# Two transformer layers on one core: key transfers spread over the cross batches, and the last mixture's rows normalised ahead

## Chip, cores, metric

One core of a Trainium2 chip runs the whole kernel in one launch. The metric is device time in microseconds, the median of several runs. The profile is one execution.

## What is computed

Two layers on a residual stream of 4 batches x 512 tokens x 256 features, all in fp32 (the matmuls that need it are done in three passes over a high and a low part). Each sub-layer adds to x what it computes from the normalised x:

```python
x = x + L0_attention(layernorm(x))            # causal, 16 heads of 16
x = x + L0_geglu(layernorm(x), ctx_1024)
x = x + L0_mixture(layernorm(x))              # 8 experts, top 2, one shared
x = x + L1_attention(layernorm(x))            # full, 16 heads of 16
x = x + L1_cross_attention(layernorm(x), ctx_1024)   # softmax over the QUERIES, for each key
x = x + L1_mixture(layernorm(x))              # 8 experts, top 2, width 1024
```

The change concerns the last two. In the cross attention the softmax runs along the query axis, so the sums belong to keys, and each key's value row is divided by its sum before the product with the probabilities. The mixture first needs logits of all 2048 normalised tokens:

```python
logits = x @ gate_w.T        # 2048 x 8
routing_weights, selected = phi_routing(logits)
```

## The kernel before

Five sub-programs (blocks) follow one another with a barrier between them. Layer 1's full and cross attention are one block, `attention(nc, "l1a", ...)`, with eight batches: b = 0 to 3 full, b = 4 to 7 cross. The mixture is `moe(nc, "l1m", ...)`.

**Attention.** The order of work is a list of steps written out by hand: `attention_schedule` yields (step, b, g, j), and each engine runs through this one list and does what it has for each step, in that order; semaphores do the rest. A step that waits holds back all that its engine has behind it. A batch has four groups g of four heads and 32 score steps "S", at = 8g + j. In a cross batch (`cross_slot`) a score step is:
- TensorE (line 937): scores of a head pair, 128 keys x 512 queries, into one of three score buffers; VectorE (`key_max`, L747): two maxima; ScalarE (L814): two exponentials with their sums.
- Every second step ("W"): VectorE inverts four sums (L756), POOL scales 64 value columns with them (`scale_v`, L612), and some steps later TensorE multiplies probabilities and scaled values ("PV", L962).

Beside these, a slot prepares the next batch: normalisation ("LN1" statistics and, on POOL, the power of the variance; "LN2" normalised rows on VectorE, L653, and on POOL the output bias added to x, `bias`, L575), projections into queries, keys and values ("PREP", "EVAC"), and stacking. Scores are computed with three fp32r operands stacked on the partitions (high, high, low), so each head's 16 rows of queries and keys are copied three times by DMA within on-chip memory: queries by SP's queue ("STACK", L516, 12 DMAs a group), keys by POOL's queue ("KEYS", `stack`, L586, 3 DMAs a head, 12 a group). A group's stack may be overwritten once the scores of the same group of the batch before are done.

In the cross batches the KEYS of the next batch's groups 0, 1 and 2 stand at steps 19 to 30, and group 3's at steps 0 to 3 of the batch itself.

**Mixture.** `moe_schedule` is such a list too. In layer 1 it begins with fillers ("IDLE": `keep_warm`, L98, products of ones that nobody reads), then, batch by batch, "LN1"/"LN2" (DVE L1853, L1859, L1865; POOL L1722, L1725), "TURN" (TensorE transposes the rows, L1959, ScalarE copies them; SP stores them for the later gather) and "LOGITS" (L1969), with fillers in between. Then VectorE routes: L2116 is its first instruction, and all of the rest depends on it. The normalised rows `xn` lie in `raw13`, the buffer that the experts' weights come into later.

## Time and profile before

| | us |
|---|---|
| median of 3 runs | 1621.8 (1618.25 to 1626.14) |
| the profiled execution's own time | 1623.72 |
| its span | 1621.9 |
| busy TensorE / VectorE / ScalarE / POOL | 1440.5 / 1178.2 / 899.5 / 627.7 |
| layer 1's cross batches | 950 to 1173 |
| start of layer 1's mixture | 1185.5 |

The span is from the first to the last instruction of the profiled execution. Shares of the whole say little here, since each block has another limit; what counts is which engine is waited for in the two stretches at the end of the table.

### The profile page before, as it was taken

What the parts mean: (1) busy time and instruction counts of PE and PEld (TensorE: products, weight loads), DVE (VectorE), ACT (ScalarE), POOL (GpSimd) and SP (SyncE); (2) the same over time, 40 slices, a digit from 0 to 9 for tenths busy, and PEclk for the clock granted to TensorE, in tenths of its full rate; (3) what the DMA queues carried; (4) which work ended last, traced back from release to release, by engine and by line L of the source; (5) the groups of instructions that cost most, each with busy time, mean ns of one, the idle gap of its engine ahead of it and who ended that gap; (6) DMA issues with size and microseconds to landing.
All of it is one profiled execution on the core that took longest, in us unless ns stands there. A gap on an engine that the chain in (4) does not pass through costs nothing. (4 is left out here: it accounts for less than half of the span.)

```text
span 1621.9 us, 30209 instructions
## 1 busy us (share of the span) xinstructions
PE 1440.5 (89%) x9918; PEld 995.4 (61%) x9918; DVE 1178.2 (73%) x2499; ACT 899.5 (55%) x1704; POOL 627.7 (39%) x917
## 2 busy tenths in 40 slices
PE   7899998989899999689999988988756899999996
PEld 3455454569899998333434332333244899999996
DVE  4767662554778888478878758888858688888884
ACT  1455553223256666046666687878812576767673
POOL 6445430010235655546445546457113232333221
PEclk8899998998999999779999998999987999999998
DMA  6223320120259886533223323223034677887872
GB/s 167 61 47 58 60 41 27 54 102 21 105 166 254 254 238 172 134 81 60 52 46 68 60 53 80 50 57 76 1 105 131 210 236 238 240 237 234 250 231 43
DMA packets 104553, 194.59 MB, mean 120 GB/s; under 512 B 30448, under 2 KB 55920, under 8 KB 101456
## 3 DMA queue, kind: packets, MB, share of 16 engines
q1 hardware_dynamic: 70864, 153.31, 30.1%
q0 software_dynamic: 33024, 38.97, 13.8%
q8 instruction: 79, 1.29, 0.3%
...
q10 hardware_dynamic: 512, 0.40, 0.1%
...
## 5 line engine op out<-in xcount | busy, mean ns | idle before, releaser
L814 ACT ACTIVATE l1a_sb_probs<-l1a_s_ps,l1a_sb_kmax 128x512 f32<-128x512 f32 x256 | 172.5, 707 | 26.7 <-DVE l1a_sb_kmax L747 25.9
L747 DVE TENSOR_REDUCE l1a_sb_kmax<-l1a_s_ps 128x1 f32<-128x512 f32 x256 | 160.7, 677 | 34.1 <-PE l1a_s_ps L937 33.2
L712 DVE TENSOR_REDUCE l1a_sb_mx<-l1a_s_ps 128x2 f32<-128x1024 f32 x128 | 153.3, 1218 | 38.5 <-PE l1a_s_ps L898 38.4
L820 ACT ACTIVATE l1a_sb_probs<-l1a_s_ps 128x1024 f32<-128x1024 f32 x128 | 130.1, 1024 | 80.0 <-PE l1a_s_ps L937 79.7
L586 POOL DMA_DIRECT2D l1a_sb_kst<-l1a_sb_hi x252 | 124.7, 499 | 101.4 <-PE l1a_s_ps L937 96.3
L937 PEld LDWEIGHTS l1a_s_ps<-l1a_sb_qst,l1a_sb_kst 49*128 49x128 f32 (+1 forms) x512 | 48.7, 189 | 168.6 <-issue 96.7
L707 DVE CUSTOM_DVE_ANT_0 l0a_sb_seen<-l0a_s_ps,l0a_sb_above 128x128 f32<-128x128 f32 (+3 forms) x256 | 113.5, 487 | 52.2 <-PE l0a_s_ps L898 51.8
L2026 PE MATMUL l1m_g_ps<-l1m_sb_rows_hi,l1m_sb_hi 128*128 128x256 f32 x512 | 146.8, 287 | 0.0
L2026 PE MATMUL l1m_g_ps<-l1m_sb_rows_lo,l1m_sb_hi 128*128 128x256 f32 x512 | 145.3, 284 | 0.0
L2026 PE MATMUL l1m_g_ps<-l1m_sb_rows_hi,l1m_sb_lo 128*128 128x256 f32 x512 | 145.3, 284 | 0.0
L937 PE MATMUL l1a_s_ps<-l1a_sb_qst,l1a_sb_kst 49*128 49x512 f32 (+1 forms) x512 | 126.3, 503 | 18.5 <-ACT l1a_sb_probs L814 16.5
L1759 POOL DMA_INDIRECT out_x<-l1m_sb_late,l1m_sb_add_to x39 | 64.5, 1654 | 187.8 <-DVE l1m_sb_late L1946 182.9
L1898 DVE TENSOR_TENSOR l1m_sb_lo<-l1m_sb_raw,l1m_sb_hi 128x512 fp32r<-128x512 f32 x184 | 119.5, 692 | 18.8 <-ACT l1m_sb_hi L1809 17.4
L820 ACT ACTIVATE l0a_sb_probs<-l0a_s_ps 128x1024 f32<-128x1024 f32 (+3 forms) x128 | 88.8, 701 | 63.7 <-PE l0a_s_ps L907 63.4
L2026 PE MATMUL l0m_g_ps<-l0m_sb_rows_hi,l0m_sb_hi 128*128 128x256 f32 x384 | 113.7, 296 | 7.4 <-DVE l0m_sb_rows_lo L1892 6.8
L2026 PE MATMUL l0m_g_ps<-l0m_sb_rows_hi,l0m_sb_lo 128*128 128x256 f32 x384 | 111.7, 291 | 0.0
L2026 PE MATMUL l0m_g_ps<-l0m_sb_rows_lo,l0m_sb_hi 128*128 128x256 f32 x384 | 111.6, 291 | 0.0
L1809 ACT ACTIVATE l1m_sb_hi<-l1m_sb_raw 128x512 fp32r<-128x512 f32 x184 | 104.7, 621 | 0.0
L2026 PE MATMUL l1m_y_ps<-l1m_sb_hi,l1m_sb_h_hi 128*128 128x256 f32 x312 | 91.0, 292 | 11.2 <-DVE l1m_sb_lo L1904 7.2
L2026 PEld LDWEIGHTS l1m_g_ps<-l1m_sb_rows_hi,l1m_sb_hi 128*128 128x128 f32 x512 | 98.8, 193 | 0.8 <-DVE l1m_sb_rows_lo L1892 0.6
L2026 PEld LDWEIGHTS l1m_g_ps<-l1m_sb_rows_hi,l1m_sb_lo 128*128 128x128 f32 x512 | 98.8, 193 | 0.0
L2026 PEld LDWEIGHTS l1m_g_ps<-l1m_sb_rows_lo,l1m_sb_hi 128*128 128x128 f32 x512 | 98.6, 193 | 0.0
...
## 6 DMA issues: line engine op xcount, KB each, us to landing
...
l1a_sb_qst<-l1a_sb_hi SPq DMA_DIRECT2D x256, 32.0 KB, 2.2
...
l0a_sb_qst<-l0a_sb_hi SPq DMA_DIRECT2D x128, 32.0 KB, 2.3
l1a_sb_qst<-l1a_sb_lo SPq DMA_DIRECT2D x128, 32.0 KB, 2.2
...
```

The lines of the kernel that those rows point to most:

```text
L586: pool.dma_start(in_stack(kst, p, e, n), in_part(source, i, p, e)).then_inc(kstacked[p], 16)
L707: ins = dve.tensor_tensor_reduce(seen[:, j % 2, e, 0:last], buffer("A", b, g, j)[:, e, 0:last], above[:, T - last:T], 1.0, -3e38, ALU.add, ...
L712: dve.tensor_reduce(mx[:, g, qt, 2 * p:2 * p + 2], buffer("A", b, g, j)[:, :, :], AX.X, ALU.max).then_inc(a_max.sem, 1)
L747: dve.tensor_reduce(kmax[:, n % 4, e:e + 1], buffer("S", b, g, j)[:, e, :], AX.X, ALU.max, negate=True).then_inc(kmax_done.sem, 1)
L814: ins = act.activation(probs[:, n % 8, e, :], at[:, e, :], ACT.Exp, bias=kmax[:, n % 4, e:e + 1], accum_out=zsum[:, n % 4, e:e + 1])
L820: act.activation(probs[:, n % 8, :, c0:T], at[:, :, c0:T], ACT.Exp, scale=SCALE).then_inc(exp_done.sem, 1)
L937: ins = pe.matmul(at[:, e, c0:T], kst[rows, p, kt * P:(kt + 1) * P], qst[rows, p, c0:T], start=True, stop=not causal)
L1759: pool.indirect_dma_start(total, bass.IndirectOffsetOnAxis(ap=at, axis=0), y[:, e % 2, t, :], None, compute_op=ALU.add).then_inc(stored[e ...
L1809: ins = act.activation(two_chunks(hi, s % 2, f), raw13[:, s % n13, f, n, :, :], ACT.Copy)
L1898: ins = dve.tensor_tensor(two_chunks(lo, s % 2, f), raw13[:, s % n13, f, n, :, :], two_chunks(hi, s % 2, f).bitcast(F32), ALU.subtract)
L2026: ins = pe.matmul(at, s, m, start=n == 0, stop=n == len(passes) - 1)
```

## The change

1. **Keys.** For the cross batches that follow a cross batch (b = 5, 6, 7), group 0's key stack is issued by SP (new `keys_stack`, own semaphores `kfirst_sp`), between its query stacks 0 and 1. Group 1's heads stay on POOL, at steps 19 to 22 of the batch before; groups 2 and 3 go to steps 4, 6, 8, 9 and 10 to 13 of the batch itself.
2. **Rows ahead.** In the last cross batch, at steps 2, 10 and 18, VectorE takes the statistics of batches 0, 1 and 2 of x (which are final there), and POOL computes the power and the normalised rows, written where the mixture expects them (`raw13` is now allocated ahead of the attention).
3. **Mixture.** Its schedule normalises batch 3 alone, starts with 6 fillers in place of 12, and has none of the others (7, 4, 4 and 4); transpositions and logits are ordered 0, 1 | 0 | 2 | 1, 2 | 3 | 3. `Tally` only moves up in the file.

```diff
@@ cross_slot
         if at == 19 and nxt is not None:
             yield "STACK", nxt, 0, 0
+            yield from keys(nxt, 0)
             yield "STACK", nxt, 1, 0
...
-        if at < GH:
-            yield "KEYS", b, NG - 1, at
-        if at >= 19 and nxt is not None and at < 19 + 3 * GH:
-            yield "KEYS", nxt, *divmod(at - 19, GH)
+        if nxt is None and at in (2, 10, 18):
+            yield "AHEAD", at // 8, 0, 0
+        if turned:
+            if at < GH:
+                yield "KEYS", b, NG - 1, at
+        elif b > 0 and kinds[b - 1] == "cross" and at in (4, 6, 8, 9, 10, 11, 12, 13):
+            yield "KEYS", b, *((2, (4, 6, 8, 9).index(at)) if at < 10 else (3, at - 10))
+        if nxt is not None and 19 <= at < 19 + GH:
+            yield "KEYS", nxt, 1, at - 19
@@ attention: SP
+            def keys_stack(b, g, head):
+                if not by_sp(b, g):
+                    return
+                p, e = 2 * g + head // 2, head % 2
+                hi_done.wait(sp, b, 1)
+                lo_done.wait(sp, b, 1)
+                s_ready.wait(sp, b - 1, 8 * g + 7)
+                for n, source in enumerate((hi, hi, lo)):
+                    sp.dma_start(in_stack(kst, p, e, n), in_part(source, 1, p, e)).then_inc(kfirst_sp[p], 16)
@@ attention: POOL
-                if b == 0 and g == 0 and e:
+                if b == 0 and g == 0 and e or by_sp(b, g):
                     return
...
+            def norm_ahead(i, *_):
+                if normed is None:
+                    return
+                stats_ahead.wait(pool, i, 2 * NT - 1)
+                pool.tensor_tensor(rstd_a[:, i, 0, :], mv_a[:, i, :, 1], const["eps"][:, :], ALU.add
+                                   ).then_inc(rstd_ahead.sem, 1)
+                rstd_ahead.wait(pool, i, 0)
+                pool.tensor_tensor(rstd_a[:, i, 1, :], rstd_a[:, i, 0, :], const["minus_half"][:, :], ALU.pow
+                                   ).then_inc(rstd_ahead.sem, 1)
+                rstd_ahead.wait(pool, i, 1)
+                for t in range(NT):
+                    pool.tensor_scalar(normed[:, i, t, :], x[:, i * NT + t, :], mv_a[:, i, t, 0:1],
+                                       rstd_a[:, i, 1, t:t + 1], ALU.subtract, ALU.mult).then_inc(normed_ahead.sem, 1)
@@ attention: VectorE
+            def stats_of(i, *_):
+                if normed is None:
+                    return
+                x_added.wait(dve, B + i, 1)
+                for t in range(NT):
+                    dve.bn_stats(stats_a[:, i, t, :], x[:, i * NT + t, :]).then_inc(stats_ahead.sem, 1)
+                stats_ahead.wait(dve, i, NT - 1)
+                dve.memset(nothing[:, :], 0.0)
+                for t in range(NT):
+                    dve.bn_aggr(mv_a[:, i, t, :], stats_a[:, i, t, :]).then_inc(stats_ahead.sem, 1)
@@ moe_schedule, layer 1 (AHEAD = 3)
-    yield "IDLE", 20 if shared else 12, 0
-    yield "LN1", 0, 0
-    yield "LN1", 1, 0
-    yield "LN2", 0, 0
-    yield "TURN", 0, 0
-    yield "LN1", 2, 0
-    yield "LN2", 1, 0
+    yield "IDLE", 20 if shared else 6, 0
...
-        yield "IDLE", 7, 0
+        for b in range(AHEAD, B):
+            yield "LN1", b, 0
+            yield "LN2", b, 0
+        yield "TURN", 0, 0
         yield "TURN", 1, 0
         yield "LOGITS", 0, 0
-        yield "IDLE", 4, 0
-        yield "LN1", 3, 0
-        yield "LN2", 2, 0
         yield "TURN", 2, 0
         yield "LOGITS", 1, 0
-        yield "IDLE", 4, 0
-        yield "LN2", 3, 0
+        yield "LOGITS", 2, 0
         yield "TURN", 3, 0
-        yield "LOGITS", 2, 0
-        yield "IDLE", 4, 0
         yield "LOGITS", 3, 0
@@ moe
+        def normed(eng, b):
+            if b >= ahead:
+                xn_done.wait(eng, b - ahead, NT - 1)
```

What the lists of instructions say, at three places. First POOL, from the end of b = 4 into b = 5: `vscaled` are the scaled values, `kst` the key stacks, `l1a_sb_v` the values' bias, `x_sb` with `l1a_sb_bo` the output bias on x (sizes are partitions x columns). Before:

```order
L612 TENSOR_TENSOR l1a_sb_vscaled<-l1a_sb_v,l1a_sb_rzsum 128x4x16
L622 TENSOR_TENSOR l1a_sb_v<-l1a_sb_v,l1a_sb_bv 128x512
L586 DMA l1a_sb_kst<-l1a_sb_hi 16x512 x2
L586 DMA l1a_sb_kst<-l1a_sb_lo 16x512
L586 DMA l1a_sb_kst<-l1a_sb_hi 16x512 x2
L586 DMA l1a_sb_kst<-l1a_sb_lo 16x512
L612 TENSOR_TENSOR l1a_sb_vscaled<-l1a_sb_v,l1a_sb_rzsum 128x4x16
L575 TENSOR_TENSOR x_sb<-x_sb,l1a_sb_bo 128x1024
L586 DMA l1a_sb_kst<-l1a_sb_hi 16x512 x2
L586 DMA l1a_sb_kst<-l1a_sb_lo 16x512
L612 TENSOR_TENSOR l1a_sb_vscaled<-l1a_sb_v,l1a_sb_rzsum 128x4x16
L586 DMA l1a_sb_kst<-l1a_sb_hi 16x512 x2
```

and in the change:

```order
L654 TENSOR_TENSOR l1a_sb_vscaled<-l1a_sb_v,l1a_sb_rzsum 128x4x16
L664 TENSOR_TENSOR l1a_sb_v<-l1a_sb_v,l1a_sb_bv 128x512
L654 TENSOR_TENSOR l1a_sb_vscaled<-l1a_sb_v,l1a_sb_rzsum 128x4x16
L617 TENSOR_TENSOR x_sb<-x_sb,l1a_sb_bo 128x1024
L654 TENSOR_TENSOR l1a_sb_vscaled<-l1a_sb_v,l1a_sb_rzsum 128x4x16 x2
L628 DMA l1a_sb_kst<-l1a_sb_hi 16x512 x2
L628 DMA l1a_sb_kst<-l1a_sb_lo 16x512
L654 TENSOR_TENSOR l1a_sb_vscaled<-l1a_sb_v,l1a_sb_rzsum 128x4x16
L628 DMA l1a_sb_kst<-l1a_sb_hi 16x512 x2
L628 DMA l1a_sb_kst<-l1a_sb_lo 16x512
L654 TENSOR_TENSOR l1a_sb_vscaled<-l1a_sb_v,l1a_sb_rzsum 128x4x16
```

The transfers that stood between the scalings are gone from here; the first ones left stand behind the bias on x and two further scalings.

Second POOL, in b = 7 of the change around step 10 (before, only scalings stand here):

```order
L654 TENSOR_TENSOR l1a_sb_vscaled<-l1a_sb_v,l1a_sb_rzsum 128x4x16
L628 DMA l1a_sb_kst<-l1a_sb_hi 16x512 x2
L628 DMA l1a_sb_kst<-l1a_sb_lo 16x512
L672 TENSOR_TENSOR l1a_sb_rstd_a<-l1a_sb_mv_a,const_eps 128x4
L675 TENSOR_TENSOR l1a_sb_rstd_a<-l1a_sb_rstd_a,const_minus_half 128x4
L679 TENSOR_SCALAR l1m_sb_raw<-x_sb,l1a_sb_mv_a,l1a_sb_rstd_a 128x256 x4
L628 DMA l1a_sb_kst<-l1a_sb_hi 16x512 x2
L628 DMA l1a_sb_kst<-l1a_sb_lo 16x512
L654 TENSOR_TENSOR l1a_sb_vscaled<-l1a_sb_v,l1a_sb_rzsum 128x4x16
L628 DMA l1a_sb_kst<-l1a_sb_hi 16x512 x2
L628 DMA l1a_sb_kst<-l1a_sb_lo 16x512
L628 DMA l1a_sb_kst<-l1a_sb_hi 16x512 x2
```

Add, power and four normalisations stand ahead of the transfers of steps 10 to 12 and of the scalings of steps 11 and 13.

Third TensorE, from the first instruction of layer 1's mixture: `const_ones_b` are fillers, `l1m_t_ps` transpositions, `l1m_y_ps` logits (written x8 here, each of 16 passes in the trace). Before:

```order
L98 MATMUL l1m_g_ps<-const_ones_b 128x512 x12
L1959 MATMUL l1m_t_ps<-const_ident,l1m_sb_raw 128x128 x8
L98 MATMUL l1m_g_ps<-const_ones_b 128x512 x7
L1959 MATMUL l1m_t_ps<-const_ident,l1m_sb_raw 128x128 x8
L1969 MATMUL l1m_y_ps<-l1m_sb_router,l1m_sb_late 128x8 x8
L98 MATMUL l1m_g_ps<-const_ones_b 128x512 x4
L1959 MATMUL l1m_t_ps<-const_ident,l1m_sb_raw 128x128 x8
L1969 MATMUL l1m_y_ps<-l1m_sb_router,l1m_sb_late 128x8 x8
L98 MATMUL l1m_g_ps<-const_ones_b 128x512 x4
L1959 MATMUL l1m_t_ps<-const_ident,l1m_sb_raw 128x128 x8
L1969 MATMUL l1m_y_ps<-l1m_sb_router,l1m_sb_late 128x8 x8
L98 MATMUL l1m_g_ps<-const_ones_b 128x512 x4
```

and in the change:

```order
L112 MATMUL l1m_g_ps<-const_ones_b 128x512 x6
L2019 MATMUL l1m_t_ps<-const_ident,l1m_sb_raw 128x128 x16
L2029 MATMUL l1m_y_ps<-l1m_sb_router,l1m_sb_late 128x8 x8
L2019 MATMUL l1m_t_ps<-const_ident,l1m_sb_raw 128x128 x8
L2029 MATMUL l1m_y_ps<-l1m_sb_router,l1m_sb_late 128x8 x16
L2019 MATMUL l1m_t_ps<-const_ident,l1m_sb_raw 128x128 x8
L2029 MATMUL l1m_y_ps<-l1m_sb_router,l1m_sb_late 128x8 x8
```

All fillers but the first six are gone, the first transpositions are 16 in a row, and the second logits 16.

## Rows read from the trace of the kernel before

**Rows 1.** Stretches, cross batches: busy us (instructions) by engine, clock (1.00 is full), DMA.

```profile
core 0: us, PE busy (x) PEld busy (x) DVE busy (x) ACT busy (x) POOL busy (x), PEclk, DMA share, GB/s
...
1006.86:1024.94 18.08, 12.64 (x68) 4.99 (x72) 12.49 (x26) 13.51 (x40) 14.92 (x28) 0.81 0.35 90
1063.40:1082.95 19.55, 12.74 (x68) 5.01 (x72) 13.54 (x26) 13.75 (x40) 16.36 (x30) 0.83 0.35 84
1024.94:1037.65 12.71, 12.34 (x70) 4.49 (x68) 12.54 (x24) 11.63 (x35) 0.89 (x3) 1.00 0.07 15
...
1120.95:1135.90 14.95, 12.16 (x60) 4.14 (x64) 10.21 (x20) 13.38 (x40) 11.64 (x25) 0.77 0.30 67
1135.90:1151.55 15.65, 13.57 (x66) 5.01 (x65) 11.14 (x23) 11.48 (x35) 0.88 (x3) 0.78 0.01 2
1151.55:1161.69 10.14, 7.51 (x46) 2.59 (x50) 9.99 (x21) 9.73 (x30) 1.17 (x4) 1.00 0.00 0
```

**Rows 2.** Waits, 950 to 1175 us: who waited <- for whom: us in total, times, longest.

```profile
PE l1a_o_ps L962 <- POOL l1a_sb_vscaled L612: 13.9, 8, 3.2
```

**Rows 3.** Timeline, POOL: start us, us, line, operation, tiles, count.

```profile
1006.02 1.05 POOL L586 DMA_DIRECT2D l1a_sb_kst<-l1a_sb_hi  x2
...
1007.57 0.30 POOL L612 TENSOR_TENSOR l1a_sb_vscaled<-l1a_sb_v,l1a_sb_rzsum 128x64 f32<-128x64 f32 x1
...
1012.25 0.31 POOL L612 TENSOR_TENSOR l1a_sb_vscaled<-l1a_sb_v,l1a_sb_rzsum 128x64 f32<-128x64 f32 x1
```

**Rows 4.** Timeline, PE; in brackets the idle time before and its releaser.

```profile
1008.02 1.06 PE L962 MATMUL l1a_o_ps<-l1a_sb_probs,l1a_sb_vscaled 128*32 128x512 f32 x8 [1.86 <-POOL l1a_sb_vscaled L612]
...
1012.70 1.93 PE L962 MATMUL l1a_o_ps<-l1a_sb_probs,l1a_sb_vscaled 128*32 128x512 f32 x8 [2.73 <-POOL l1a_sb_vscaled L612]
```

**Rows 5.** Timeline, DVE, the same stretch.

```profile
1015.40 1.29 DVE L747 TENSOR_REDUCE l1a_sb_kmax<-l1a_s_ps 128x1 f32<-128x512 f32 x2 [2.72 <-PE l1a_s_ps L937]
```

**Rows 6.** Timeline, DVE, where the mixture's logits are read.

```profile
1205.60 0.29 DVE L2116 TENSOR_TENSOR l1m_sb_lg<-l1m_y_ps,l1m_sb_rbias 128x128 f32<-128x128 f32 x1 [7.61 <-PE l1m_y_ps L1969]
```

**Rows 7.** Groups, POOL, 950 to 1174 us: count, busy us, mean ns of one, idle before.

```profile
L575 POOL TENSOR_TENSOR x_sb<-x_sb,l1a_sb_bo 128x1024 f32<-128x1024 f32 x2 | 4.7, 2350 | 0.0
L554 POOL TENSOR_TENSOR l1a_sb_rstd<-l1a_sb_rstd,const_minus_half 128x4 f32<-128x4 f32 x2 | 2.1, 1032 | 0.2
```

**Rows 8.** Groups, DVE, 1185 to 1206 us.

```profile
L1853 DVE BATCH_NORM_STATS2 l1m_sb_stats<-x_sb 128x6 f32<-128x256 f32 x16 | 5.6, 408 | 4.3 <-PEq L304 4.3
...
L1859 DVE BATCH_NORM_AGGREGATE l1m_sb_mv<-l1m_sb_stats 128x2 f32<-128x6 f32 x16 | 1.5, 156 | 0.2
```

**Rows 9.** Timeline, PE, two projections of b = 7.

```profile
1133.43 1.99 PE L989 MATMUL l1a_m_ps<-l1a_sb_wout,l1a_sb_ox 128*128 128x256 f32 x8
...
1145.27 3.78 PE L989 MATMUL l1a_m_ps<-l1a_sb_wout,l1a_sb_ox 128*128 128x256 f32 x8
```

**Rows 10.** Timeline, PE, head of layer 1's mixture.

```profile
1185.49 5.09 PE L98 MATMUL l1m_g_ps<-const_ones_b 128*128 128x512 bf16 x12 [4.99 <-PEq L304]
...
1196.83 1.04 PE L1959 MATMUL l1m_t_ps<-const_ident,l1m_sb_raw 128*128 128x128 f32 x8
1197.70 1.85 PE L1969 MATMUL l1m_y_ps<-l1m_sb_router,l1m_sb_late 128*128 128x8 f32 x16
1199.41 1.02 PE L98 MATMUL l1m_g_ps<-const_ones_b 128*128 128x512 bf16 x4
1200.27 1.04 PE L1959 MATMUL l1m_t_ps<-const_ident,l1m_sb_raw 128*128 128x128 f32 x8
```

**Rows 11.** Timeline, PE, logits of three batches in layer 0's mixture.

```profile
371.68 7.69 PE L1969 MATMUL l0m_y_ps<-l0m_sb_router,l0m_sb_xnT 128*128 128x8 f32 x48
```

**Rows 12.** Stretches around those logits; columns as in rows 1.

```profile
371.06:374.47 3.41, 3.41 (x33) 3.41 (x31) 1.26 (x2) 1.23 (x2) 0.00 (x0) 1.00 0.00 0
374.47:377.89 3.42, 3.42 (x18) 3.42 (x18) 0.12 (x1) 0.00 (x0) 0.00 (x0) 0.50 0.00 0
```

**Rows 13.** Stretches, head of layer 1's mixture; columns as in rows 1.

```profile
1190.00:1196.00 6.00, 5.63 (x42) 4.20 (x41) 5.92 (x27) 2.17 (x4) 2.66 (x5) 0.98 1.07 366
```

More of the change, by code:

```diff
@@ L87, in wait, with __init__ @@
             eng.wait_ge(self.sem, value)
+class Tally:
+    def __init__(self, sem, per=1):
+        self.sem, self.per = sem, per
+    def wait(self, eng, n, step=0):
+        value = n * self.per + step + 1
+        if value > 0:
+            eng.wait_ge(self.sem, value)
 CHUNK = (0, 2, 1, 3)
+AHEAD = 3
 def keep_warm(pe, at, const, n):
@@ L288, in attention_schedule, with attention @@
         yield "ADD", b, g, j
-def attention(nc, tag, x, const, stages):
+def attention(nc, tag, x, const, stages, normed=None):
     kinds = [kind for kind, _ in stages for _ in range(B)]
@@ L359, in attention @@
         nothing = sb("nothing", [P, 1])
+        if normed is not None:
+            stats_a, mv_a, rstd_a = sb("stats_a", [P, AHEAD, NT, 6]), sb("mv_a", [P, AHEAD, NT, 2]), sb("rstd_a", [P, AHEAD, 2, NT])
         one_row = sb("one_row", [1, T], F32R)
@@ L408, in attention @@
         x_biased = steps("x_biased", 1)
+        stats_ahead, rstd_ahead, normed_ahead = (Tally(sem(n), per) for n, per in (
+            ("stats_ahead", 2 * NT), ("rstd_ahead", 2), ("normed_ahead", NT)))
         kmax_done = steps("kmax_done", 0, 2 * 8 * NG)
@@ L460, in product, with by_sp @@
             return m_ps[:, :] if b else buffer("PREP", b, use, 0)[:, 0, :]
+        kfirst_sp = [sem(f"kfirst_sp{p}") for p in range(2)] if has_cross else None
         STACKED = 6 * 16
+        def by_sp(b, g):
+            return g == 0 and b > 0 and kinds[b - 1] == "cross"
         def kstack_in(eng, b, p):
+            if by_sp(b, p // 2):
+                eng.wait_ge(kfirst_sp[p], (b - B) * STACKED)
+                return
             eng.wait_ge(kstacked[p], (b + 1) * STACKED - (STACKED // 2 if p < 2 else 0))
@@ L541, in _ @@
                              ).then_inc(ones_in, 16)
-            run({"STACK": stack, "LN1": before_batch, "CTX": context, "M": rows})
+            run({"STACK": stack, "KEYS": keys_stack, "LN1": before_batch, "CTX": context, "M": rows})
         @block.gpsimd
@@ L1254, in halves_to @@
     return sum(halves(n) for n in range(e % 2, e + 1, 2))
-class Tally:
-    def __init__(self, sem, per=1):
-        self.sem, self.per = sem, per
-    def wait(self, eng, n, step=0):
-        value = n * self.per + step + 1
-        if value > 0:
-            eng.wait_ge(self.sem, value)
 ALL, TOKENS, WEIGHTS = slice(0, 5), slice(0, 2), slice(2, 5)
@@ L1496, in sem @@
             return ctx.enter_context(nc.semaphore(f"{tag}_{name}"))
-        raw13, raw2 = sb("raw13", [P, n13, NF, 2, CC, 2 * P]), sb("raw2", [P, n2, FC, D])
+        if shared:
+            raw13 = sb("raw13", [P, n13, NF, 2, CC, 2 * P])
+        raw2 = sb("raw2", [P, n2, FC, D])
+        ahead = 0 if shared else AHEAD
         hi1, lo1, hi3, lo3 = (sb(n, [P, 2, CC, width], F32R) for n in ("hi1", "lo1", "hi3", "lo3"))
@@ L1861, in normal @@
             def normal(b, _):
-                ln_stats.wait(dve, b, 2 * NT - 1)
-                ln_rstd.wait(dve, b, 1)
+                ln_stats.wait(dve, b - ahead, 2 * NT - 1)
+                ln_rstd.wait(dve, b - ahead, 1)
                 for t in range(NT):
@@ L1954, in turn @@
             def turn(b, _):
-                xn_done.wait(pe, b, NT - 1)
+                normed(pe, b)
                 for c in range(CC):
@@ L2273, in build @@
         moe(nc, "l0m", x, const, of("l0m"), 512, phi=False, shared=True)
-        attention(nc, "l1a", x, const, [("full", of("l1a")), ("cross", of("l1x") | context)])
-        moe(nc, "l1m", x, const, of("l1m"), 1024, phi=True, shared=False, out=out)
+        raw13 = ctx.enter_context(nc.sbuf_tensor("l1m_sb_raw13", [P, 1, 4, 2, CC, 2 * P], F32))
+        normed = raw13[:, 0, :, :, :, :].rearrange("p f n c d -> p f (n c) d")
+        attention(nc, "l1a", x, const, [("full", of("l1a")), ("cross", of("l1x") | context)], normed)
+        moe(nc, "l1m", x, const, of("l1m"), 1024, phi=True, shared=False, out=out, raw13=raw13)
 def rope_factor():
```

31 lines of the change are left out of this document (19 added, 12 removed).

## Prediction

> **What bounds the kernel now.** I read the profile in this order: busy time and clock by stretch, the waits, the timelines of single engines, and the groups of instructions for prices.
>
> The change touches two places of layer 1: the four cross batches of attention (b = 4 to 7, from 950 us to 1173 us; each is 32 steps of scores, in four quarters of 8) and the first 20 us of the mixture (from 1185.5 us). In a cross batch VectorE and ScalarE share the bound: a quarter that nothing disturbs (from 1024.94 us) takes 12.71 us, of which DVE is busy 12.54 and ACT 11.63 [rows 1]. The first quarters of b = 5 and b = 6 take 18.08 and 19.55 us with the same DVE and ACT work (12.49 and 13.54 us of DVE), and there POOL is busy 14.92 and 16.36 us against 0.89 us in the quiet quarter [rows 1]. The waits say who is late: TensorE waits 13.9 us for POOL's scaled values [rows 2]. The timeline gives the chain: POOL works without a pause on key transfers, each issue some half a microsecond, so that one scaling of 0.3 us stands at 1007.57 us behind three issues and the next only at 1012.25 us [rows 3]. TensorE, in its own order, stands 1.86 us and then 2.73 us before the product that reads it [rows 4]; the scores queued behind that product are late, and DVE stands 2.72 us [rows 5]. Note that the first wait of 1.86 us starved nobody: some 2 us are hidden by the three score buffers. In these stretches the granted clock is 0.81 and 0.83, where the quiet quarter has 1.00 [rows 1].
>
> At the head of the mixture nothing but TensorE and the normalisation runs: DVE gets the logits at 1205.60 us, 20.1 us after the start, and had stood 7.61 us for them; the whole routing follows from there [rows 6]. So this piece is on the path with its full length.
>
> **Part 1, keys.** For b = 5, 6, 7 group 0's 12 issues go to SP, and groups 2 and 3 (24 issues) go from steps 27 to 3 to steps 4 to 13; group 1 goes four steps earlier. SP then issues 60 stack transfers in a batch where it had 48, behind query stack 0 and ahead of query stacks 1 and 2. At about 0.6 us of issue each (the estimate is from the half microsecond of POOL's [rows 3], taken higher) that is 36 us in a batch of 50 us or more, and group 1's queries are wanted 8 steps into the next batch: I cost SP at nothing; its cover is the 14 us left.
> POOL's queue in the first steps becomes: scaling, the bias on x, two scalings. The bias waits for DVE's normalised rows and takes 2.35 us [rows 7]; the scaling behind it comes about 1 us late, less than what is hidden. So I take both first quarters to the undisturbed length. DVE there: 8 steps of 1.27 us (10.14 us for the 8 steps of the last batch's third quarter, which holds nothing else [rows 1]) and the normalisation of 2.2 us, 12.3; I take 13.0, since the quiet quarters need 12.7.
> - b = 5: 18.08 to 13.0, -5.1 us. b = 6: 19.55 to 13.0, -6.5 us.
> - b = 7, first quarter: 14.95 us now [rows 1]; without the stall 10.1 to 10.7.
> Steps 8 to 13 now hold six heads, 6 x 1.44 us of issue and 3 x 0.3 us of scaling = 9.5 us, beside about 8.5 us of DVE: POOL is 1 us late at most, again hidden.
>
> **Part 2, rows of three batches normalised in b = 7.** DVE gains at steps 2, 10 and 18 four statistics of 0.41 us and four aggregates of 0.16 us (issued closely, together 1.85 us, as at the mixture's head) [rows 8]: 5.6 us on the engine that bounds. POOL gains the add, a power of 1.03 us [rows 7] and four normalisations of 128x256. The trace has none of these on POOL. Below they are bounded by the scaling of 64 elements, 0.3 us [rows 3], above by the bias of 1024 elements, 2.35 us [rows 7]; I take 0.6 us, a quarter of the latter, since 256 elements are a quarter. A block on POOL is then 0.2 + 1.03 + 2.4 = 3.7 us, and the scaling behind it 2.5 us late; at step 10 one head's transfers follow, so there it is about 4 us late. I put 1 us on that.
> - b = 7, first quarter: 10.2 + 1.85 = 12.1, from 14.95: -2.9 us.
> - second: DVE 10.2 + two additions to x of 0.6 + 1.85 = 13.3 us. Now it takes 15.65 us at clock 0.78, since a projection of 1.99 us at full clock took 3.78 us at half [rows 9]. That loss of some 4 us may or may not come again; TensorE will be less busy there than before, so I keep it: 17.5, +1.9 us.
> - third: 10.14 to 12.0, +1.9 us. Fourth: as before.
> Sum of the attention: -5.1 - 6.5 - 2.9 + 1.9 + 1.9 + 1.0 = -9.7 us. Bounds: -15 (no half-clock stretch in b = 7, POOL never late) and -3 (two more such stretches of 3 to 4 us).
>
> **Part 3, head of the mixture.** Now the first transposition waits for DVE and POOL (statistics, power, normalisation), and 12 fillers of together 5.09 us keep TensorE running. The change starts transposing after 6 fillers and has no filler after that. At full clock a batch costs: transpositions 0.87 us, logits 1.71 us, fillers 0.86 us (differences of starts) [rows 10]. The new chain is 6 fillers at half clock (half of 5.09, so 2.5), four times (0.87 + 1.71) = 10.3, and one wait for ScalarE's copy before the last logits, 0.85 (its place was under a filler): 13.7 us at full clock, against 20.1. But the clock starts at half, and the logits do not hold it: in layer 0 the same logits, three batches in a row, ran from 371.68 us at full clock up to 374.47 and at half clock from there though TensorE was 100% busy, and took 7.69 us; 2.8 us of it at full clock are 1.6 batches, so the other 1.4 took 4.9 us, 3.5 us a batch [rows 11, 12]. All at half: 2.5 + 4 x 1.74 + 4 x 3.5 + 0.85 = 24.3 us, +4.2. Every microsecond at full clock takes one off. The clock rose some 4.9 us after the start before (0.98 from 1190.00 us on [rows 13]); I let it do the same, and fall some 3 us after logits begin to dominate (at 6.0 us), so 4 us at full: 20.3 us, and call the piece +0.2. The normalisation of the fourth batch (done 5 us after the start) and the stores of rows lie beside this.
> Here a rule speaks against the change. The Trainium skill, page "TensorE: Matmul & The Clock Gate", part 4 on the transposition, says that transpositions don't count as TensorE activity in the way matmuls do, so that the full clock doesn't engage on them. By that, the head would be all at half clock, the first rival below. The trace neither proves nor refutes it: in the mixture's head transpositions always stand next to fillers.
>
> **Sum.** -9.7 + 0.2 = -9.5 us. The profiled execution took 1623.7 us (span 1621.9), so it would take 1614.2. The median of the three runs is 1621.8, 1.9 below it: 1612.3, say 1612. A measurement of this kernel tells about 0.5%, 8 us, from no change, so this stands close to that bound.
>
> **The rivals.**
> - *The head stays at half clock throughout* (+4.2 instead of +0.2): for it, the logits' fall and the absence of fillers; against it, that TensorE has no pause in the first 6 us of the new chain, 6 fillers and two batches' transpositions. Time 1616. Chance 0.17.
> - *The head holds the full clock from 4.9 us on*: 4.9 us at half do 4.9 us of cold work, the rest is halved: 24.3 - 0.85 - 4.9 = 18.5, halved 9.3; 15.1 us, -5.0. For it, that each batch's transpositions interrupt the logits. With it -14.5 us, 1607; if b = 7 escapes its half-clock stretch, 1603. Chance 0.15.
> - *The stall stays* (the change doesn't do what it says): the late scaling is then due to the bias on x, which waits for DVE's rows in the same place, and not to the transfers. Against it: the scaling at 1007.57 stood ahead of that bias and was late already [rows 3]. Then only part 2's additions, +3 to +5, against some relief at b = 7: 1621. Chance 0.08.
> - *Slower: POOL's normalisations block the scalings of b = 7.* If one takes not 0.6 but up to the 2.35 us of the upper bound, a block is 0.2 + 1.03 + 9.4 = 10.6 us; less the 3 us hidden, TensorE and then DVE stand 7.6 us, three times: +23 us in place of the +1.0, sum +12.5, 1634. It turns the forecast into no gain from about 1.5 us a normalisation. For it, a power over 4 elements takes 1.03 us, so POOL's prices aren't by elements alone; against it, both tensor operations shown scale with elements. Chance 0.08.
> - The forecast itself has 0.52.
>
> **Numbers.** The forecast's own range is 1605 to 1619 (bounds of part 2 and the half-clock stretches). With the rivals up to a fifth left out: 1603 to 1621. Faster by over 0.5% (below 1613.7): six tenths of the forecast, all of the second rival, a fifth of the first and a little for a lucky b = 7: 0.55. Slower: the POOL rival and a little of the others, 0.09. The rest, 0.36.
>
> **What would show it.** In the profile after: POOL's share in the first quarters of b = 5 and 6 falls from 15 us to about 5, TensorE's wait for the scaled values from 13.9 us to 3 or less, and those quarters take 13 us. In b = 7 three statistics blocks of 1.85 us on DVE, POOL's normalisations at 0.6 us each. From the mixture's start to DVE's reading of the logits some 20 us, with the clock's share telling which of the three cases of the head it was. It is wrong if TensorE still waits over 5 us for the scaled values, if DVE stands more than 3 us behind any of the three blocks, or if the head is under 17 us.

## The result, and the profile after

The changed kernel takes 1628.99 us (median of 20 runs, 1620.96 to 1635.57) against 1620.78 us for the kernel before (20 runs, 1614.35 to 1630.9). The ratio is 1.0046 with a 95% interval of 1.0032 to 1.0059: about 7.5 us slower. Forecast were 1612 us, 9.5 us faster. The profiled execution took 1631.8 us (span 1630.0, mean clock 0.93).

The table splits the two profiled spans at the same places (the start of each cross batch on VectorE, its last maximum, TensorE's first instruction in the mixture, the reading of the logits), in us:

| piece | before | after | difference | forecast |
|---|---|---|---|---|
| up to b = 4 | 949.93 | 948.82 | -1.1 | 0 |
| b = 4 | 56.93 | 56.90 | 0 | 0 |
| b = 5 | 56.54 | 53.32 | -3.2 | -5.1 |
| b = 6 | 57.55 | 54.09 | -3.5 | -6.5 |
| b = 7 | 52.56 | 71.58 | **+19.0** | +1.9 |
| end of attention to mixture | 11.98 | 8.92 | -3.1 | 0 |
| head of the mixture | 20.10 | 20.86 | +0.8 | +0.2 |
| the rest | 416.32 | 415.54 | -0.8 | 0 |
| span | 1621.9 | 1630.0 | +8.1 | -9.5 |

So the keys' part brought less than forecast, and b = 7 took back more than all other pieces gained together. The stretches of the changed kernel, with the columns of [rows 1]; the first two are the first quarters of b = 5 and 6, the other four are all of b = 7:

```profile
1005.72:1020.57 14.85, 11.82 (x64) 4.84 (x64) 11.67 (x26) 13.39 (x40) 7.96 (x14) 0.89 0.34 80
1059.05:1075.17 16.12, 14.69 (x68) 5.83 (x64) 11.61 (x25) 14.73 (x43) 8.61 (x15) 0.68 0.34 82
1113.13:1132.52 19.39, 13.66 (x60) 4.93 (x63) 11.87 (x29) 14.26 (x42) 12.76 (x20) 0.65 0.22 46
1132.54:1154.59 22.05, 12.81 (x66) 4.71 (x61) 12.78 (x32) 10.78 (x31) 14.82 (x25) 0.77 0.13 26
1154.59:1172.17 17.58, 10.17 (x46) 3.45 (x50) 11.66 (x31) 11.90 (x35) 7.47 (x11) 0.71 0.00 1
1172.17:1184.71 12.54, 10.43 (x58) 2.81 (x58) 11.23 (x22) 9.82 (x29) 0.88 (x3) 0.86 0.00 0
```

POOL's 14.92 and 16.36 us in the first two have become 7.96 and 8.61, and the wait of [rows 2] is gone there: that part of the chain was read rightly. In b = 7 POOL's time stands in its place, and all four quarters show a clock below full. What the profile puts down as TensorE's waits for scaled values lies in b = 7 alone (5.66 us at its step 10, the rest at its end):

```profile
PE l1a_o_ps L1031 <- POOL l1a_sb_vscaled L654: 7.8, 4, 5.7
```

POOL's groups over the cross batches (columns of [rows 7]):

```profile
L679 POOL TENSOR_SCALAR l1m_sb_raw<-x_sb,l1a_sb_mv_a,l1a_sb_rstd_a 128x256 f32<-128x256 f32 x12 | 14.6, 1226 | 0.3
...
L675 POOL TENSOR_TENSOR l1a_sb_rstd_a<-l1a_sb_rstd_a,const_minus_half 128x4 f32<-128x4 f32 x3 | 3.1, 1034 | 0.2
```

A normalisation of 128x256 takes 1.23 us, where the forecast had 0.6. What this does is best seen in the second block. First POOL's timeline, start and duration first:

```profile
1138.68 0.20 POOL L672 TENSOR_TENSOR l1a_sb_rstd_a<-l1a_sb_mv_a,const_eps 128x4 f32<-128x4 f32 x1 [0.80 <-DVE l1a_sb_mv_a L825]
1138.95 1.03 POOL L675 TENSOR_TENSOR l1a_sb_rstd_a<-l1a_sb_rstd_a,const_minus_half 128x4 f32<-128x4 f32 x1
1140.10 4.85 POOL L679 TENSOR_SCALAR l1m_sb_raw<-x_sb,l1a_sb_mv_a,l1a_sb_rstd_a 128x256 f32<-128x256 f32 x4
1144.89 1.09 POOL L628 DMA_DIRECT2D l1a_sb_kst<-l1a_sb_hi  x2
1145.98 0.49 POOL L628 DMA_DIRECT2D l1a_sb_kst<-l1a_sb_lo  x1
1146.48 0.31 POOL L654 TENSOR_TENSOR l1a_sb_vscaled<-l1a_sb_v,l1a_sb_rzsum 128x64 f32<-128x64 f32 x1
```

The block holds POOL from 1138.68 to 1144.95 us, and one head's transfers follow in its order; only at 1146.48 comes the scaling. TensorE in the same stretch:

```profile
1146.93 1.94 PE L1031 MATMUL l1a_o_ps<-l1a_sb_probs,l1a_sb_vscaled 128*32 128x512 f32 x8 [5.66 <-POOL l1a_sb_vscaled L654]
1148.80 3.42 PE L1058 MATMUL l1a_m_ps<-l1a_sb_wout,l1a_sb_ox 128*128 128x256 f32 x8
```

It stands 5.66 us, and the projection behind it, 1.99 us at full clock [rows 9], takes 3.42. The scores are queued behind the projection. VectorE, next:

```profile
1152.70 1.29 DVE L804 TENSOR_REDUCE l1a_sb_kmax<-l1a_s_ps 128x1 f32<-128x512 f32 x2 [9.23 <-PE l1a_s_ps L1006]
```

9.23 us without work on an engine that bounds the batch. The blocks of steps 2 and 18 do the same on a smaller scale: TensorE stands 3.74 and 3.72 us, VectorE 4.35 and 4.52. POOL's scaling behind the block of step 2, and TensorE's product that reads it:

```profile
1125.92 0.30 POOL L654 TENSOR_TENSOR l1a_sb_vscaled<-l1a_sb_v,l1a_sb_rzsum 128x64 f32<-128x64 f32 x1
1126.32 1.94 PE L1031 MATMUL l1a_o_ps<-l1a_sb_probs,l1a_sb_vscaled 128*32 128x512 f32 x8 [3.74 <-ACT l1a_sb_probs L883]
```

The profile names ScalarE here, because an exponential ends in the same hundredth (1126.23 us) as the scaling (1126.22). By the code the product waits only for the exponentials of steps 0 and 1, so it is the scaling. TensorE's waits behind the three blocks are thus 5.66 + 3.74 + 3.72 = 13.1 us.

The mixture's head, TensorE's timeline and then the stretches at each level of the clock (0.50 is 1.2 GHz, 1.00 is 2.4 GHz):

```profile
1193.63 2.72 PE L112 MATMUL l1m_g_ps<-const_ones_b 128*128 128x512 bf16 x6 [1.93 <-PEq L324]
1196.15 3.61 PE L2019 MATMUL l1m_t_ps<-const_ident,l1m_sb_raw 128*128 128x128 f32 x16
1199.60 1.85 PE L2029 MATMUL l1m_y_ps<-l1m_sb_router,l1m_sb_late 128*128 128x8 f32 x16
...
1202.21 6.18 PE L2029 MATMUL l1m_y_ps<-l1m_sb_router,l1m_sb_late 128*128 128x8 f32 x32
```

```profile
1193.63:1199.52 5.89, 5.89 (x22) 3.92 (x23) 3.17 (x13) 1.67 (x3) 1.23 (x2) 0.50 0.59 189
1199.52:1202.93 3.41, 3.41 (x34) 3.41 (x32) 0.00 (x0) 1.68 (x4) 0.00 (x0) 1.00 1.05 352
1202.93:1214.49 11.56, 10.83 (x51) 10.34 (x50) 0.00 (x1) 1.32 (x3) 0.00 (x0) 0.50 0.48 167
```

This is what the forecast drew: full clock for 3.4 us (forecast 4), fallen under the logits, 20.86 us in all (forecast 20.3). It is one execution, though. The same head took 20.85 us in ahead_only, 18.58 in doubled and 16.43 in spread (runs of the next section), where the clock was full in it for 3.4, 6.8 and 9.1 us.

### The profile page after: what moved, and what is told of

Read it like the earlier page. It is cut to its first block and busy times, and to the rows that moved or that the text cites. A ratio compares the mean times of both kernels' runs of the same rounds, so it can differ in the third digit from the quotient of the medians.

```text
span 1630.0 us, 30142 instructions
## 1 busy us (share of the span) xinstructions
PE 1446.9 (89%) x9893; PEld 1000.5 (61%) x9893; DVE 1172.1 (72%) x2487; ACT 902.1 (55%) x1704; POOL 626.1 (38%) x893
## 5 line engine op out<-in xcount | busy, mean ns | idle before, releaser
L628 POOL DMA_DIRECT2D l1a_sb_kst<-l1a_sb_hi x228 | 113.1, 500 | 104.1 <-PE l1a_s_ps L1006 96.3
```

The lines of the kernel that those rows point to most:

```text
L628: pool.dma_start(in_stack(kst, p, e, n), in_part(source, i, p, e)).then_inc(kstacked[p], 16)
```

## The experiments

Two theories stood against each other. **Theory 1:** POOL's blocks of four normalisations hold up the scalings of b = 7. **Theory 2:** b = 7 is longer because its own keys' transfers now stand at steps 4 to 13 beside the scalings. Every run below was compared with the kernel before on the same chip; the length of b = 7 comes from the profiled execution (before 52.56 us, the changed kernel 71.58).

### The parts apart: keys_only and ahead_only

keys_only is the changed kernel without the rows ahead; the mixture is as before:

```diff
-        if nxt is None and at in (2, 10, 18):
-            yield "AHEAD", at // 8, 0, 0
...
-        ahead = 0 if shared else AHEAD
+        ahead = 0
```

> The stacked keys' transfers are placed as in the change, the mixture and its normalisations are as before. Theory 1 (the three blocks of 4 normalisations on POOL, 4.85 us each, hold up the scalings of the last batch): without them the last batch is back at or under the 52.6 us it had before, the first quarters of b=5 and b=6 keep their 3.2 and 3.4 us, and the time is 7 to 10 us under the kernel before, ratio 0.994 to 0.996. Theory 2 (the last batch is longer because its own keys' transfers are now issued by POOL at steps 4 to 13 beside the scalings): the last batch stays near 71.6 us, and the time is about 12 us over the kernel before (+19 less 6.6), ratio 1.007.

Measured: ratio 0.9932 (0.9906 to 0.9958), 11 us faster than before (theory 1: 7 to 10). b = 7 takes 48.64 us, b = 5 and 6 take 53.30 and 54.09. Its stretches, the first quarters of b = 5, 6 and 7 and the second of b = 7:

```profile
1003.53:1018.36 14.83, 11.81 (x64) 4.86 (x64) 11.68 (x26) 13.37 (x40) 7.94 (x14) 0.88 0.34 80
1056.83:1072.94 16.11, 14.68 (x67) 5.83 (x64) 11.60 (x25) 14.70 (x43) 8.61 (x15) 0.68 0.37 81
1110.92:1125.02 14.10, 12.12 (x60) 3.94 (x62) 10.40 (x20) 14.00 (x42) 6.02 (x13) 0.76 0.29 61
1125.02:1137.61 12.59, 10.51 (x66) 3.67 (x64) 11.14 (x23) 10.79 (x33) 9.34 (x21) 1.00 0.24 48
```

With the transfers where the change puts them, b = 7 is 3.9 us shorter than before, not longer. Theory 2 falls.

ahead_only is the reverse: keys as before, rows ahead as in the change.

> The mixture's part of the change alone: keys' transfers are placed as before, POOL normalises three batches of rows within the last attention batch. Theory 1: the last batch is longer by about 19 us less what the keys' placement gave or cost there (16 to 22 us), 3 us come back between attention and mixture, the head is 0.8 us longer: 13 to 20 us over the kernel before, ratio 1.008 to 1.012. Theory 2: the last batch is within 2 us of 52.6, and the time 2 to 3 us under the kernel before.

Measured: ratio 1.0145 (1.0113 to 1.0176), 23 us slower than before, a little above theory 1's 13 to 20. b = 7 takes 72.02 us (+19.5), the head 20.85. The 3 us between attention and mixture did not come back: that piece is 12.03 us. So they belong to the keys' part, which neither theory had; keys_pool below takes this up. The two parts add up to +12 us, the whole change measured +7.5; with six executions each, their intervals are 4 and 5 us wide to either side, so this is no sign that they act on each other.

### The price on POOL: doubled

```diff
-                for t in range(NT):
+                for k in range(2 * NT):
+                    t = k % NT
+                    normed_ahead.wait(pool, i, k - NT)
```

> The changed kernel with each of the 12 normalisations on POOL done twice, 8 in a block, the same numbers written again. Theory 1: each block is 4.85 us longer and PE's waits for scaled values grow by about as much: the last batch is 12 to 17 us longer than 71.6, the kernel 12 to 17 us over the changed one (ratio to the kernel before 1.012 to 1.015). Theory 2: the block is not what is waited for, the last batch is within 3 us of 71.6 and the ratio stays near 1.005.

Measured: ratio 1.0125 (1.0087 to 1.0164), b = 7 at 84.44 us, +12.9 on the changed kernel for 14.4 us more of POOL. The group of POOL and TensorE's largest wait in it:

```profile
L681 POOL TENSOR_SCALAR l1m_sb_raw<-x_sb,l1a_sb_mv_a,l1a_sb_rstd_a 128x256 f32<-128x256 f32 x24 | 29.0, 1227 | 0.3
```

```profile
PE l1a_o_ps L1033 <- POOL l1a_sb_vscaled L654: 27.6, 4, 10.2
```

TensorE's waits behind the three blocks are 8.56, 10.17 and 8.54 us, 14.2 more than the changed kernel's, and nine tenths of what is added to the blocks is added to the batch. Theory 1 holds in size too.

This profile shows something else. In it the clock stayed full in the first quarters of b = 5 and 6, ahead of the batch that the edit touches:

```profile
1007.52:1021.00 13.48, 10.52 (x68) 4.42 (x64) 11.47 (x27) 13.48 (x40) 8.12 (x14) 1.00 0.43 99
1059.47:1072.95 13.48, 10.52 (x68) 4.41 (x64) 11.46 (x26) 13.48 (x40) 8.13 (x14) 1.00 0.44 100
```

13.48 us is thus what these quarters take at full clock, and ScalarE is busy for all of it.

### The same work in small pieces: spread

```diff
-                for t in range(NT):
-                    pool.tensor_scalar(normed[:, i, t, :], x[:, i * NT + t, :], ...
+            def norm_one(i, t, *_):
+                pool.tensor_scalar(normed[:, i, t, :], x[:, i * NT + t, :], ...
...
+        if nxt is None and at in (14, 15, 16, 17, 19, 20, 21, 22, 24, 25, 26, 27):
+            yield "NORM", *divmod((14, 15, 16, 17, 19, 20, 21, 22, 24, 25, 26, 27).index(at), NT), 0
```

> The changed kernel with the 12 normalisations as steps of their own, one each at steps 14 to 17, 19 to 22 and 24 to 27 of the last batch; the blocks at steps 2, 10 and 18 keep the statistics and the two small operations. Theory 1: POOL is never taken for more than 1.2 us at a time, so that the waits for scaled values stay under 1 us, the last batch is within 4 us of 52.6 and the time 6 to 10 us under the kernel before, ratio 0.994 to 0.996. Theory 2: the sum of POOL's work in the batch is the same, the last batch stays above 65 us and the ratio near 1.004.

Measured: ratio 0.9955 (0.9927 to 0.9982), about 7 us faster than before and 15 us faster than the change (0.9955 against 1.0046). The same 12 instructions of 1.22 us are there:

```profile
L682 POOL TENSOR_SCALAR l1m_sb_raw<-x_sb,l1a_sb_mv_a,l1a_sb_rstd_a 128x256 f32<-128x256 f32 x12 | 14.6, 1224 | 0.0
```

```profile
PE l1a_o_ps L1034 <- POOL l1a_sb_vscaled L656: 3.1, 4, 1.4
```

TensorE's longest wait for scaled values fell from 5.7 us to 1.4 (expected under 1). But b = 7 takes 58.90 us, not within 4 us of 52.6: theory 1 says nothing of this rest. The next two take it apart. Another execution of the same attention code (spread_fillers, below) has b = 7 at 56.67 us, so lengths of b = 7 from single profiles can stand 2 us apart without any change.

### VectorE's share: stats_only and stats_dve

stats_only is keys_only with the blocks at steps 2, 10 and 18 but no normalisation in them; stats_dve has no operation of POOL in them either. In both the mixture does its own work, and the extra results go unused.

```diff
@@ stats_only: norm_ahead on POOL
-                rstd_ahead.wait(pool, i, 1)
-                for t in range(NT):
-                    pool.tensor_scalar(normed[:, i, t, :], x[:, i * NT + t, :], mv_a[:, i, t, 0:1],
-                                       rstd_a[:, i, 1, t:t + 1], ALU.subtract, ALU.mult).then_inc(normed_ahead.sem, 1)
@@ stats_dve: the add and the power out too
-                stats_ahead.wait(pool, i, 2 * NT - 1)
...
+                return
```

> keys_only with the statistics of three batches on DVE and POOL's two small operations at steps 2, 10 and 18 of the last batch, without the 12 normalisations; the mixture does its own, so these results go unused. It tells what of the last batch's growth is DVE's and what POOL's. If DVE's 2.2 us a block count in full and POOL's blocks are all the rest: the last batch is 5 to 7 us over the 48.65 us of keys_only, the time 5 to 7 us over it (ratio 0.996 to 0.998). If POOL's 1.2 us of small operations, or the waits they bring, hold up the scalings too: the last batch is 9 us or more over it.

> stats_only without POOL's two small operations in each block: only DVE's statistics (8 instructions, 2.2 us a block) are left in the last batch, their results unused. In stats_only the batch was 57.66 us, 9.01 over the 48.65 us of keys_only, where DVE's own work is 3 times 2.2, 6.6 us. If it is DVE's time and the half clock that follows from it: within 1 us of 57.7 us. If POOL's wait for the statistics and its 1.23 us are what makes the rest: 54 to 56 us.

Measured: stats_only 0.9954 (0.9931 to 0.9977), b = 7 at 57.66 us; stats_dve 0.9951 (0.9929 to 0.9973), b = 7 at 56.01. The second quarter of b = 7 in each:

```profile
1123.72:1140.77 17.05, 13.09 (x66) 4.83 (x65) 12.80 (x32) 11.10 (x33) 10.68 (x23) 0.80 0.18 37
```

```profile
1123.30:1140.11 16.81, 13.26 (x66) 4.88 (x65) 12.79 (x31) 11.08 (x33) 9.43 (x21) 0.80 0.19 38
```

In keys_only it took 12.59 us at clock 1.00. The statistics (1.73 us from their first start to the next instruction's, in each block) put 1.65 us on VectorE here and 4.2 us on the quarter. The clock stands at half in 6.8 us of it, and the projection takes longer (3.60 us). The run warm, below, has no statistics but happened to have half clock in 6.8 us of the same quarter:

```profile
1118.00:1133.63 15.63, 13.55 (x66) 5.08 (x65) 11.13 (x22) 11.62 (x35) 9.35 (x21) 0.78 0.21 40
```

So 3.0 of the 4.2 us are what half clock costs, and 1.2 are VectorE's own. All four kernels that have statistics but no blocks of normalisations show a long second quarter (stats_only, stats_dve, spread, spread_fillers: 16.63 to 17.05 us, 3.4 to 6.8 of them at half clock); keys_only, keys_again and keys_pool do not (12.59). That the statistics bring the half clock is read from this pattern; no run held the clock with the statistics in place. The expectations put their work at 2.2 us a block, which was too much. From 48.64 us (keys_only) the batch grows in steps that add up to the changed kernel's:

| in b = 7 | b = 7 | step |
|---|---|---|
| keys alone | 48.64 | |
| + statistics on DVE (3 x 1.73 us) | 56.01 | +7.4 |
| + add and power on POOL | 57.66 | +1.7 |
| + 12 normalisations in blocks (the change) | 71.58 | +13.9 |
| (the same 12 one at a time: spread) | 58.90 | +1.2 |

Of these, +1.7 and +1.2 lie within the 2 us by which two executions of one code differ, so neither is shown to be more than nothing. The +7.4 is seen alike in four kernels (56.01 to 58.90 us with the statistics, 47.67 to 50.32 in the five without them), and +13.9 stands clear. In time, the two runs must be held against the set of their own chip: stats_only is 0.0022 of the ratio above keys_only (3.6 us), stats_dve 0.0068 above keys_again (11 us).

### SP's share and the end of attention: keys_pool

```diff
-        if nxt is not None and 19 <= at < 19 + GH:
-            yield "KEYS", nxt, 1, at - 19
+        if nxt is not None and kinds[b] == "cross" and 19 <= at < 19 + 2 * GH:
+            yield "KEYS", nxt, *divmod(at - 19, GH)
...
-            return g == 0 and b > 0 and kinds[b - 1] == "cross"
+            return False
```

> keys_only with no transfer of keys on SP: groups 0 and 1 of the next batch go to POOL's queue at steps 19 to 22 and 23 to 26, groups 2 and 3 stay at steps 4 to 13 of their own batch. Theory 1 (it is the 3 of 4 groups that POOL issued ahead in steps 19 to 30 before that made the scalings at a batch's start late; two groups there already leave POOL free by the batch's end): the first quarters stay within 1 us of keys_only (14.8, 16.1, 14.1 us), the time within 3 us of keys_only. Rival (SP's share is needed): the first quarters are 2 us or more longer each, as POOL issues 12 transfers more in steps 19 to 26. On the end of attention: POOL's closing drain took 9.22 us where POOL issued all 156 transfers of keys of this part and 3.83 us where it issued 120. If the number of its transfers sets it, it is near 9.22 us here and the mixture starts up to 3 us later than in keys_only; if their place does, it is 3.83 us.

Measured: ratio 0.9942 (0.9919 to 0.9964), no different from keys_only (0.9932). The first quarters, shorter than keys_only's by 1.0 to 2.0 us where the clock stood higher (1.00, 0.88, 0.87 against 0.88, 0.68, 0.76):

```profile
1001.34:1014.88 13.54, 10.58 (x68) 4.41 (x64) 11.45 (x25) 13.54 (x40) 8.20 (x14) 1.00 0.37 85
1053.34:1067.50 14.16, 11.98 (x68) 4.85 (x64) 11.49 (x25) 13.67 (x40) 8.22 (x14) 0.88 0.36 79
1105.53:1118.65 13.12, 10.98 (x60) 3.89 (x62) 10.17 (x20) 13.07 (x39) 5.79 (x13) 0.87 0.20 41
```

So SP's share isn't needed for them: what counted was to have the late groups out of POOL's queue at the turn of the batch. The end of attention shows what SP's share does buy. TensorE's first instruction in the mixture, first in keys_pool, then in keys_only:

```profile
1165.24 1.01 PE L112 MATMUL l1m_g_ps<-const_ones_b 128*128 128x512 bf16 x2 [5.04 <-PEq L321]
```

```profile
1169.33 1.02 PE L112 MATMUL l1m_g_ps<-const_ones_b 128*128 128x512 bf16 x4 [1.93 <-PEq L322]
```

Between attention and mixture all engines meet, and each closes with a DRAIN. The sequencer's record of POOL's, from the traces, with the transfers of keys that POOL issued from 940 us on (a few records are missing; by the code they are 36 apart):

```
                 key transfers recorded on POOL   DRAIN starts   us
before                     165                      1175.16     9.22
ahead_only                 164                      1194.30     9.22
keys_pool                  160                      1154.86     9.22
after                      127                      1186.36     3.83
keys_only                  124                      1161.20     3.83
spread                     124                      1170.26     3.83
```

Where POOL issues all transfers, its DRAIN takes 9.22 us, and in the kernel before it ends at 1184.38 us, 3.15 us after the last addition to x (1181.23); with a quarter of those of three batches on SP it takes 3.83 us and is done before that addition. keys_pool has the new places but all on POOL, and 9.22: so it is their number on POOL's queue, not their place. That explains 3.1 us of the result.

### The clock: warm, warm2, keys_again, spread_fillers

warm puts one matmul of ones into the score buffer ahead of the scores of some steps; warm2 adds the second quarter of b = 7; keys_again is keys_only once more, on the chip of warm2.

```diff
                 c0, at = first_col(kt), buffer("S", b, g, j)
+                if cross and (b > B and g == 0 and j < 6 or b == B and g == 2 and j < 4
+                              or b == NB - 1 and g == 1):
+                    keep_warm(pe, at[:, 0, :], const, 1)
```

> keys_only with one matmul of ones (128x512, its result overwritten) ahead of each of the first six key-score steps of b=5, 6 and 7, and of four in the third quarter of b=4, where the granted clock fell to 0.5 within 4 us after the quarter began. If half clock makes up what the first quarters have over 13.5 us (14.83, 16.11 and 14.11 in keys_only; 13.47 and 13.48 where the clock stayed full): the clock stays full there and 3 to 6 us are gained on keys_only, ratio 0.989 to 0.992. If PE's extra 22 matmuls of 0.22 us each lie on the path, or the clock falls all the same: within 2 us of keys_only or up to 5 us over it.

> warm with a matmul of ones ahead of each of the eight key-score steps of the last batch's second quarter too, where in warm the clock was at half from 1124.55 to 1131.38 us and the quarter took 15.63 us, not 12.6. If the clock is what lengthened it: full clock from b=4 to the mixture, the quarter at 12.6 to 13.2 us, and 5 to 8 us under keys_again (about 1602 us, ratio 0.988 to 0.991). If the clock falls in another place instead: within 3 us of keys_again.

> keys_only once more, beside the next kernel: 0.993 to 0.995 of the kernel before, and the last batch at 48.7 us where the granted clock is at half in 6.8 us of it.

Measured: warm 0.9912 (0.9877 to 0.9948; one of its eight executions took 2425 us, no profile shows why, and it isn't in the ratio), warm2 0.9898 (0.9872 to 0.9923), keys_again 0.9883 (0.9858 to 0.9909). The first quarters of b = 5 and 6 and all of b = 7 in warm2:

```profile
1001.66:1015.79 14.13, 12.07 (x73) 4.83 (x69) 11.47 (x26) 13.57 (x40) 8.15 (x14) 1.00 0.37 94
1054.26:1068.38 14.12, 12.06 (x73) 4.83 (x69) 11.46 (x26) 13.56 (x40) 8.15 (x14) 1.00 0.41 95
1106.55:1119.51 12.96, 11.55 (x66) 4.17 (x68) 10.21 (x21) 12.96 (x40) 6.23 (x13) 1.00 0.30 63
1119.51:1132.60 13.09, 12.75 (x73) 4.38 (x71) 11.19 (x22) 11.47 (x35) 9.19 (x21) 1.00 0.25 48
1132.60:1145.38 12.78, 11.17 (x46) 3.58 (x50) 10.08 (x22) 11.80 (x35) 1.46 (x5) 0.64 0.00 1
```

The clock stays full where the matmuls stand, and the quarters are 14.13, 14.12 and 12.96 us against 14.83, 16.11 and 14.10; the first two are still 0.65 above the 13.48 us of full clock without the added matmuls. Then it falls in the third quarter of b = 7 instead, which takes 12.78 us and not 10.14; in warm it fell in the second (15.63, above). The four batches together take 209.5 us in warm and in warm2, 212.9 in keys_only and 208.6 in keys_again, where the clock held through b = 4 by itself. So the half-clock stretches are a real cost of the single quarters, but these matmuls don't buy a shorter kernel: the expected 5 to 8 us under keys_again didn't come. Warm's ratio lies where it was expected (0.989 to 0.992), but keys_again reached 0.9883 without such matmuls.

spread_fillers is spread with three runs of four matmuls of ones between the logits of the head.

> spread with three runs of four matmuls of ones back in the mixture's head. In the changed kernel the head took 20.86 us with full clock in 3.4 us of it, in spread 16.4 us. If the clock is what the head's length hangs on: full clock through the logits and a head of 15 to 17 us, in every run, and a time 1 to 4 us under spread's 1612.9. Rival: the fillers cost their own 12 matmuls (2.6 us at full clock) and the clock falls anyway: 1 to 4 us over spread.

Measured: 0.9952 (0.9927 to 0.9978), against spread's 0.9955: no difference. Its head took 18.21 us, spread's 16.43, the changed kernel's 20.86. The head without such matmuls isn't the same length each time (16.43 to 20.86 us in four executions), and with them it was within that; how it splits over many executions was not measured.

**The best version** is keys_only: 0.9932 and 0.9883 against the kernel before, in two sets of six executions on two chips, faster than it in both; the changed kernel stands at 1.0046. The two ratios are 8 us apart though the code is the same, so a difference of a few us between two sets of six tells little; the changed kernel's +7.5 us rests on 20 executions of each kernel. warm, warm2 and keys_pool can't be told from it; it is preferred as the simplest. The versions with statistics in b = 7 are at 0.995.

## Why the prediction was wrong

**Step that failed first: the price of a normalisation, "I take 0.6 us, a quarter of the latter".** It took 1.23 us. The interpolation went by elements from one row of an addition. A nearer row of the trace of before was left unread (groups of POOL over the whole span):

```profile
L596 POOL TENSOR_TENSOR l1a_sb_vaug<-l1a_sb_v,l1a_sb_bv 128x256 f32<-128x256 f32 x16 | 11.5, 735 | 4.1 <-ACT l1a_sb_v L775 4.0
```

Even that is the price of one operation with two tensors; this one subtracts and multiplies by two values per partition. The Trainium skill, page "GPSIMD Engine Reference", section 4.1, has operations with one input at roughly line rate and only those with two inputs about twice as slow as on VectorE; here POOL's one-input form was the slower, 1.23 against 0.735 us for the same 256 elements. The other prices of the block were right: a power of 1.03 us, an add of 0.20.

**Second: what is hidden.** The forecast let 3 us of a block vanish behind three score buffers and "put 1 us" on all three. The runs say that at most the first microsecond does: doubled adds 12.9 us for 14.4, and the blocks' normalisations cost 13.9 of their 14.6 us. Probably the cover that hid a wait of 1.86 us before [rows 4] was spent already, since the same block had first held VectorE for its statistics; no run shows this part alone. Then came the half clock (37.5 us of it in b = 7, 23.9 in stats_only) and, at step 10, the transfers queued behind the block. The slower rival had the mechanism and the place right, with a chance of 0.08. At the true price its term gives 3 x (0.2 + 1.03 + 4.9 - 3) = 9.4 us in place of the 1.0, which leaves -1.1 us of the forecast's -9.5: the price alone takes away nearly all of the gain. (Its point of reversal is, by its own term, 1.3 us a normalisation and not 1.5.) POOL's steps took 15.6 us (1.7 + 13.9), and that is the second error. Two of the forecast's own signs of being wrong came with it: TensorE waits over 5 us for scaled values, and VectorE stands more than 3 us behind each of the three blocks (4.35, 9.23, 4.52).

**Third: VectorE's statistics, +1.9 and +1.9 us.** Their work was right (1.73 us a block, forecast 1.85). They cost 7.4 us against keys_only, with half clock beside them (23.9 us of it in b = 7 of stats_dve, 6.8 in keys_only). In the third quarter keys_only takes 10.14 us, stats_dve 13.78 with 9.6 us at half, and warm2, without statistics, 12.78 with 9.3 at half: there too most of the growth is the clock's. The forecast kept the second quarter's old loss of 4 us as given; keys_only shows it gone (12.59 us at full clock).

**Fourth: b = 5 and 6, "I take 13.0".** The mechanism holds: no wait for scaled values is left there, POOL is at 8 us (forecast 5). 13.48 us is the length at full clock (doubled), and there ScalarE is busy all the time: its 13.51 and 13.75 us stood in [rows 1] already, and only DVE's work was counted. The other 1.4 and 2.6 us are half clock, which the forecast took to vanish with the wait. So -3.2 and -3.5 in place of -5.1 and -6.5. 

The first quarter of b = 7 went the same way: 14.10 us by the keys alone where 10.2 was taken, with ScalarE busy 14.00 of it. There it was the second quarter that gained, 3.1 us, by keeping its clock; warm, with the keys in the same places, has it at 15.63 us and clock 0.78, as before (15.65, 0.78). So this part of keys_only's 3.9 us hangs on where the clock falls.

**Right:** SP carries its transfers at no cost that shows: keys_pool, which has none on SP, is no faster. The head came out 0.6 us from the forecast, by the forecast's own steps, but that closeness is luck in part: with 16.43 us in spread, it could have come out near the second rival's 15.1. By the rule on transpositions (the Trainium skill, "TensorE: Matmul & The Clock Gate", part 4) it would have stayed at half clock: here the clock rose at 1199.52 us, after 3.4 us in which TensorE had run nothing but 16 of them. That doesn't prove that they count, since six matmuls of ones went before, but it speaks against the rule for 128x128 in fp32.

**Not foreseen:** the 3.1 us between attention and mixture, which no term had. And a slip: the second rival's sum is -9.7 - 5.0 = -14.7 us, not -14.5.

The sum by what was measured: -1.1 - 3.2 - 3.5 + (-3.9 + 7.4 + 1.7 + 13.9) - 3.1 + 0.8 - 0.8 = +8.2, the spans' +8.1.
